# Source blocks of a graph kernel: packing ahead, four banks for the counts, aggregation in three parts

## What is computed

```python
# layer 0, three rounds: sum over neighbours, two linear maps
agg = segment_sum(x[src], dst); h = (1 + eps[i]) * x + agg
h = relu(bn(h @ W1[i] + b1[i])); h = relu(bn(h @ W2[i] + b2[i])); x = bn(h)
# layer 1: per edge, then mean over dst
h = relu(concat([x[row], edge_attr]) @ W1 + b1) @ W2 + b2
g = relu(concat([x, scatter_mean(h, col)]) @ W3 + b3) @ W4 + b4
# layer 2: attention over edges; layer 3: typed messages, normalised
```

## Time and profile before

| | us |
|---|---|
| median of 3 runs (lowest, highest) | 2091.39 (2090.84, 2094.32) |
| the profiled execution | 2095.73 |
| its span in the trace | 2094.4 |
| TensorE busy, share of the span | 1366.7, 65% |
| GpSimd busy | 790.0, 38% |
| VectorE busy | 1133.6, 54% |
| ScalarE busy | 601.6, 29% |
| mean granted TensorE clock (1.0 is 2.4 GHz) | 0.827 |

### The profile page before, as it was taken

One profiled execution on the slowest core, in us unless ns is written; L12 is line 12 of the kernel. 1 busy time (PEld: TensorE's weight loads), 2 busy tenths in 40 slices (PEclk: granted clock), 3 DMA queues, 4 the chain that ended last, 5 costly groups with the idle time before them and its releaser, 6 DMA issues.

```text
span 2094.4 us, 49695 instructions
## 1 busy us (share of the span) xinstructions
PE 1366.7 (65%) x20608; PEld 1258.3 (60%) x20609; DVE 1133.6 (54%) x3435; ACT 601.6 (29%) x1403; POOL 790.0 (38%) x881
## 2 busy tenths in 40 slices
PE   5103200011004777777899899999799999889997
PEld 5101200010003566666689799999789999789896
DVE  8104101110003666666544756655588888888987
ACT  0000000000003565555421344444356666500000
POOL 2771777777770000000000144444000011189886
PEclk9999555555555776677799899999899999899999
DMA  7301300001013766767475578888466664244443
GB/s 223 117 14 41 106 15 15 15 14 45 14 32 142 280 266 246 269 266 266 190 285 215 199 283 313 301 313 297 170 249 236 221 250 136 99 151 169 156 175 98
DMA packets 89288, 360.78 MB, mean 172 GB/s; under 512 B 24941, under 2 KB 38432, under 8 KB 82080
## 3 DMA queue, kind: packets, MB, share of 16 engines
q1 hardware_dynamic: 75744, 349.84, 45.1%
q0 software_dynamic: 13312, 7.69, 1.6%
HBM read 250.77 MB, written 106.68 MB: 171 GB/s over the span
## 4 chain that ended last, share of the span: by engine, by line
PE 47%; another core or an unknown queue 17%; issue 13%; DVE 12%; ACT 8%; POOL 2%; DMA 1%; SPq 0%; DVEq 0%; ACTq 0%; POOLq 0%
PE ps L2573 9%; PE ps L2921 7%; PE ps L2909 5%; PE ps L3540 5%; PE ps L3187 4%; PE ps L2463 3%; ACT arena L2530 2%; PE ps L3554 2%; PE ps L700 1%; PE ps L2389 1%; DVE arena L3605 1%; ACT arena L2475 1%; PE ps L2399 1%; DVE arena L3130 1%
## 5 line engine op out<-in xcount | busy, mean ns | idle before, releaser
L2194 POOL DMA_INDIRECT recs<-arena x416 | 415.1, 998 | 203.1 <-issue 126.6
L2979 POOL CAST arena<-arena 128x512 f32<-128x512 bf16 (+1 forms) x175 | 119.2, 683 | 733.2 <-DMA arena<-hot_out 563.7
L3540 PE MATMUL ps<-arena 125*128 125x64 bf16 x5850 | 192.5, 194 | 13.2 <-issue 13.1
L3540 PEld LDWEIGHTS ps<-arena 125*128 125x128 bf16 x5850 | 186.8, 99 | 14.4 <-issue 14.0
L2463 PE MATMUL ps<-wz,arena 32*128 32x128 f32 x1248 | 83.0, 381 | 164.6 <-ACT arena L2475 89.4
L2921 PE MATMUL ps<-arena 128*128 128x125 f32 x1300 | 182.2, 282 | 0.0
L3065 DVE TENSOR_TENSOR arena<-ps,arena 128x512 f32<-128x512 f32 (+1 forms) x175 | 114.3, 653 | 118.6 <-PE ps L2909 115.6
L2463 PEld LDWEIGHTS ps<-wz,arena 32*128 32x128 f32 x1248 | 68.9, 271 | 172.6 <-ACT arena L2475 90.9
L2921 PEld LDWEIGHTS ps<-arena 128*128 128x128 f32 x1300 | 158.8, 192 | 0.0
L2369 DVE TENSOR_SCALAR arena<-iota,arena 128x128 bf16<-128x128 bf16 x650 | 127.3, 253 | 50.7 <-issue 50.7
L3012 ACT ACTIVATE arena<-arena 128x512 f32<-128x512 f32 (+1 forms) x175 | 105.1, 601 | 171.7 <-DVE arena L3065 171.7
(11 more groups left out here) (381 smaller groups left out, 2692.3 us busy)
## 6 DMA issues: line engine op xcount, KB each, us to landing
arena<-ids_out SPq DMA_DIRECT2D x100, 832.0 KB, 6.4
arena<-hot_out SPq DMA_DIRECT2D x75, 832.0 KB, 6.3
arena<-e_out SPq DMA_DIRECT2D x25, 1664.0 KB, 7.0
arena<-adj_out SPq DMA_DIRECT2D x41, 800.0 KB, 6.2
e_out<-arena SPq DMA_DIRECT2D x25, 1024.0 KB
hot_out<-arena SPq DMA_DIRECT2D x25, 832.0 KB, 6.1
adj_out<-arena SPq DMA_DIRECT2D x25, 800.0 KB, 4.4
e_out<-arena SPq DMA_DIRECT2D x25, 640.0 KB, 3.2
```

The lines of the kernel that those rows point to most:

```text
L2194: nc.gpsimd.indirect_dma_start(out=recs, out_offset=bass.IndirectOffsetOnAxis(ap=slot_row[:, t:t + 1], axis=0), in_=rec_in[:, t, :], in_of ...
L2979: nc.gpsimd.tensor_copy(hot_e[s % NH][:, 0:len(js), :], hot_in[d % 2][:, js[0]:js[0] + len(js), :])\
L3540: ins = M(bank(step % 4, C, k * C), hot_r[d % 2][r][0:NP_, j * SLOTS:(j + 1) * SLOTS], px3[:, block_of(d, j), piece, r * C:(r + 1) * C], s ...
```

## The change

The order of work inside steps 0 to 24 is altered, and the PSUM banks of the counts. No computation is added or dropped.

- ACT packs block d+1 between the copies of e1's first and second half of block d (`act_pack`), and no longer at the head of step d+1. Only block 0 is packed at the head.
- The counts' seven groups lie in banks 4, 5, 2, 3, 4, 5, 2. Groups 0 and 1 wait only for the copies of the block before, 2 and 3 for the copies of the last e1, and 4 to 6 for groups 0 to 2.
- The transposes of block d wait for two of the four copies of the last half of e1 (banks 0 and 1), not for all four.
- `pe_z` of block d-1 is cut into 6, 12 and 7 matmuls: before e1's first half, between the halves, after the second. E1's first half now waits until all counts of block d are copied, since it writes banks 2 and 3.

```diff
@@ -2198,6 +2198,7 @@
 
         OPEN = 4
         READY = 5 * CH
+        Z_CUTS = (6, 18)
         LAST_E1 = 40
         DEGREES = 36
         STEPS = 26 * 2 + NT + 6
@@ -2380,7 +2381,7 @@
                     pe.wait_ge(sem("attr_packed"), d + 1)
                     if d >= 1:
                         pe.wait_ge(sem("attr_turned"), d)
-                        pe.wait_ge(sem("e1_made"), 8 * d)
+                        pe.wait_ge(sem("e1_made"), 8 * d - 2)
                     nc.tensor.transpose(bank(0, SLOTS)[0:3 * SB, :], idt[d % 2].rearrange("p k j -> p (k j)"),
                                         ident[:, :])
                     for g, js in enumerate(groups(d)):
@@ -2392,10 +2393,14 @@
                     for g in range(7):
                         n = 7 * d + g
                         pe.wait_ge(sem("hot"), n + 1)
-                        if n >= 2:
-                            pe.wait_ge(sem("adj_made"), n - 1)
+                        if g == 0 and d:
+                            pe.wait_ge(sem("adj_made"), 7 * d - 1)
+                        if g in (2, 3) and d:
+                            pe.wait_ge(sem("e1_made"), 8 * d)
+                        if g >= 4:
+                            pe.wait_ge(sem("adj_made"), 7 * d + g - 3)
                         for k, j in enumerate(sb_tiles(g)):
-                            to = bank(4 + n % 2, SLOTS, k * SLOTS)
+                            to = bank(ADJ_BANK[g], SLOTS, k * SLOTS)
                             ins = M(to, hot_s[d % 2][:, j, :], hot_d[d % 2][:, j, :], start=True, stop=j != d,
                                     skip_group_check=True)
                             if j == d:
@@ -2403,20 +2408,25 @@
                                         skip_group_check=True)
                         if g == 6:
                             for j in range(SB):
-                                ins = M(bank(4 + n % 2, 1, 256 + j), hot_d[d % 2][:, j, :], one16[:, 0:1], start=True,
+                                ins = M(bank(ADJ_BANK[g], 1, 256 + j), hot_d[d % 2][:, j, :], one16[:, 0:1], start=True,
                                         stop=True, skip_group_check=True)
                         ins.then_inc(sem("adj_mm"), 1)
-                if step < NT - 1:
-                    pe.wait_ge(sem("attr_turned"), step + 1)
-                    pe_e1_half(pe, step, 0)
                 if 1 <= step <= NT:
                     d = step - 1
                     pe.wait_ge(sem("adj_made"), 7 * d + 7)
                     pe.wait_ge(sem("z_read"), d)
-                    pe_z(pe, 0, d, range(NT))
+                    pe_z(pe, 0, d, range(Z_CUTS[0]))
+                if step < NT - 1:
+                    pe.wait_ge(sem("attr_turned"), step + 1)
+                    pe.wait_ge(sem("adj_made"), 7 * step + 7)
+                    pe_e1_half(pe, step, 0)
+                if 1 <= step <= NT:
+                    pe_z(pe, 0, step - 1, range(Z_CUTS[0], Z_CUTS[1]))
                 if step < NT - 1:
                     pe.wait_ge(sem("e1_made"), 8 * step + 4)
                     pe_e1_half(pe, step, 1)
+                if 1 <= step <= NT:
+                    pe_z(pe, 0, step - 1, range(Z_CUTS[1], NT))
                 for l in range(3):
                     pe_tail(pe, l, step)
                 for l in (1, 2):
@@ -2451,6 +2461,8 @@
                     pe.wait_ge(sem("deg_rows"), 1)
                     pe_e1_last(pe)
 
+        ADJ_BANK = (4, 5, 2, 3, 4, 5, 2)
+
         def e1_slots(half, r):
 
             return [j for j in range(16 * half, min(16 * half + 16, SB)) if j % 4 == r]
@@ -2463,6 +2475,14 @@
                     ins = M(bank(r, HID, (g - 4 * half) * HID), attT[rows, g * 128:(g + 1) * 128],
                             wz[rows, r * HID:(r + 1) * HID], start=True, stop=True, skip_group_check=True)
             ins.then_inc(sem("e1_mm"), 1)
+
+        def act_pack(act, d):
+
+            act.wait_ge(sem(f"block_in{d % 2}"), 16 * (d // 2 + 1))
+            act.wait_ge(sem("turned"), d)
+            A(attc.rearrange("p (j f) -> p j f", f=FE),
+              recd[d % 2].rearrange("p (j f) -> p j f", f=REC)[:, :, 4:REC], ACT.Copy)\
+                .then_inc(sem("attr_packed"), 1)
 
         def act_e1_half(act, d, half):
 
@@ -2502,11 +2522,8 @@
             for step in range(STEPS):
                 if step < NT:
                     d = step
-                    act.wait_ge(sem(f"block_in{d % 2}"), 16 * (d // 2 + 1))
-                    act.wait_ge(sem("turned"), d)
-                    A(attc.rearrange("p (j f) -> p j f", f=FE),
-                      recd[d % 2].rearrange("p (j f) -> p j f", f=REC)[:, :, 4:REC], ACT.Copy)\
-                        .then_inc(sem("attr_packed"), 1)
+                    if d == 0:
+                        act_pack(act, 0)
                     act.wait_ge(sem("turned"), d + 1)
                     if d >= 2:
                         act.wait_ge(sem(f"ids_stored{d % 2}"), 16 * (d // 2))
@@ -2526,11 +2543,12 @@
                         m = len(sb_tiles(g))
                         act.wait_ge(sem("adj_mm"), n + 1)
                         if g == 6:
-                            A(present[:, d, :], bank(4 + n % 2, SB, 256), ACT.Copy)
-                        A(adj[d % 2][:, 4 * g:4 * g + m, :].rearrange("p s n -> p (s n)"), bank(4 + n % 2, m * SLOTS),
+                            A(present[:, d, :], bank(ADJ_BANK[g], SB, 256), ACT.Copy)
+                        A(adj[d % 2][:, 4 * g:4 * g + m, :].rearrange("p s n -> p (s n)"), bank(ADJ_BANK[g], m * SLOTS),
                           ACT.Copy).then_inc(sem("adj_made"), 1)
                     if d < NT - 1:
                         act_e1_half(act, d, 0)
+                        act_pack(act, d + 1)
                         act_e1_half(act, d, 1)
                 for l in range(3):
                     act_tail(act, l, step)
```

## The result

| | changed | before |
|---|---|---|
| median, same chip (lowest, highest) | 2010.35 us (2007.65, 2013.39) | 2091.11 (2090.78, 2094.32) |
| ratio, 95% interval | 0.9611 (0.9594, 0.9628) | |
| profiled execution; its span | 2007.65; 2006.3 | 2095.73; 2094.4 |
| start of block 1's transposes | 644.29 | 652.28 |
| a step, mean of 23 | 12.76 | 16.08 |

The change takes 3.9%, some 81 us, where 72 were forecast. The two profiled spans differ by 88.1 us: 8.0 before block 1, 76.3 in the 23 steps, 3.8 behind them. (In one of the five sets of runs the chip was of another kind: the kernel before takes 1655 us on it, and the change, seen there together with an earlier load alone, brings nothing. The experiments come to it.)

What follows compares the result with a forecast made beforehand. A chain across engines, PE and ScalarE taking turns, was taken to set the 16.08 us step. Summed terms gave 13.0: 23 steps save 70.8 us, the start 1.5, so 2091.39 - 72.3 = 2019.1 us; range 1996 to 2050.

Steps and rivals of the forecast that it cites:

- a step of 13.0: Steps between block 1's and block 24's transposes: 16.08 us falls to 13.0, with ends of 11.5 and 14.2.
- a sign of being wrong: In the steps: the forecast is wrong if PE's first part of the aggregation waits for VectorE's reading.
- the six aggregation matmuls: Ahead of e1's first half: six matmuls of the aggregation fill PE's wait, with no term in the step's sum.
- The packing: ScalarE's instruction between e1's copies and the transposes: 0.80 us leaves the chain, covered by 0.89 idle.
- The four banks: Copies of counts: six already run without a gap, 3.46 us; 0.58 gained at the end is given back; net nothing.
- E1's first half: PE's e1 matmuls in each step: 1.8 us, from 2.02 at the low clock to 1.42 at the high one.
- Rival A: In the steps, the block's load or VectorE becomes late: 13.9 us a step, 2039 us; chance 0.22.
- B: First block beside the scatter: e1's first matmul waits for ScalarE's copies, overlap lost, +85 us, 2104; chance 0.03.
- C: In the steps, the clock stays high: step 11.5 to 12.0, DMA and VectorE begin to bind, 1991 us; chance 0.10.
- D: In the steps, nothing happens, since another wait of the same length stands right behind; chance 0.02.
- The start: Block 1's transposes, at 652.28, could begin after two copies, at 649.98 + 0.8: 1.5 us more gained.
- 14.2: Low-clock end of the step in us, with mean tail; by the rule on cycling PSUM banks the step would go there.

## Why the prediction was right, by its own steps

**The number, and the luck in it.** The forecast had 72 us and 2019; the ratio gives 81 and 2010. The turns of PE and ScalarE that the change takes apart were the right mechanism, which undoing each part shows. But a step of 13.0 was summed over these turns alone, with VectorE 2.2 us early, and in the changed kernel VectorE's reading holds PE up in 14 of 22 steps, which the forecast itself had named as a sign of being wrong. Where that wait is gone, with the load early, the same turns give 11.76, at a clock of 0.93. So the sum was some 1.2 us too long, the wait that it left out was worth 1.0 with the clock that goes with it, and the two nearly cancel: that the step came out at 12.76 is in part luck.

**The sum of the step.** 13.0 forecast (its terms give 13.07), 12.76 measured. Its terms in the step from 784.40 to 796.95: transposes 1.1 (forecast 1.5; 1.05 was the low end); copies of them 1.1 (1.07); six copies of counts 3.0 (3.46); group 6's copies 0.4 (0.4), in part beside the six aggregation matmuls; e1's first half 2.07 (1.8); four copies 2.1 (2.06); e1's second half 0.95 (0.95); the rest until the next transposes 1.1 (1.45). One term stands there that the sum had at nothing: the six aggregation matmuls, 0.9. The transposes with the ids came out at 0.28 to 0.31 in every step but the first, so the clock was up there each time.

**Three terms mis-sized.** *The packing*: I priced it at its own 0.80 a step, 18 us, in the expectation of its run; alone it brings 53, 2.3 to 2.4 us a step. 1.1 of them are PE's shorter wait before the transposes, for part of the tail of ScalarE that stood between copies and packing (0.64) leaves the chain too. The clock rises from 0.73 to 0.86, which I take for the rest: after shorter pauses PE has its high clock more often. No run held the clock fixed, so that share is argued, not shown. The prediction's step total had both in, as a range. *The four banks*: "ScalarE gains nothing within them" was wrong. A merged row of the timeline hid the gaps: six copies take 3.01 instead of 3.46, 0.45 a step, 10 us. The chain of waits of the kernel before had shown 0.14 and a piece of PE's work after every second copy, and I should have gone by it. *E1's first half* at the high clock takes 1.17 (676.58 in the changed kernel), below my low end of 1.42, which I had scaled from the second half.

**The parts don't add.** The packing alone brings 53; the other parts without it 58; together 81. Undoing any one costs 17 to 24. With any one part missing the step is 13.6 to 13.7, at clocks from 0.76 to 0.85; with all it is 12.8, and there the late load and VectorE behind it stop it.

**Rival A** (0.22) is what happened as a mechanism, though not at its price: PE's first part waits for VectorE's reading in 14 of 22 steps. I had VectorE's reading 2.2 us early at a step of 13.0 and late only if the load grew. The load did not grow in the median (3.5 us in both kernels); what went is my slack, since the chain without VectorE is shorter than 13.0. A's price was a mean step of 13.9; nine steps are of 13.5 to 16.7 and the others 11.0 to 12.7, so that the mean stayed near the forecast. The early load took 25 us, more than the 20 between A's price and the forecast. **B** fell: ScalarE's copies come at 500.48 and 589.38 in the changed kernel, 88.9 apart (before 89.0), so PE's new wait cost nothing. **C** was not reached by the change, but the early load reached its step (11.8) and its time (1989 against 1991). The prediction's **D**, no gain, fell with the ratio.

**The start.** 1.5 us were forecast and 8.0 measured. Of these 1.3 are the change's: the transposes of block 1 start 1.0 us after e1's copies begin (643.28), before 2.3 (649.98). The other 6.7 stand in ScalarE's copies already, and 14.3 in its small copy of group 6 (500.48, before 514.77), ahead of which nothing of the change but the banks comes. Over the ten profiles of crawling chips that small copy starts anywhere from 499 to 515, whatever the kernel, and block 1 from 643.8 to 652.3. I take the 6.7 as spread.

**The clock and the banks.** The rule of the Trainium skill that I weighed (TensorE: Matmul & The Clock Gate, "A second HAM failure mode: psum-queue depth-cycling") speaks of cycling through banks. Here four banks gave the higher clock (0.88) and two the lower (0.80), with e1's added wait the only other difference, and the step did not go to 14.2. Nor does the number of banks order the clock over all runs: four banks with the aggregation in one piece have 0.76, two banks with the packing moved 0.86. So the rule is not borne out in this kernel. What makes the clock fall is not settled. From 670 to 900 us of the changed kernel it falls eleven times in some 18 steps, ten times before e1's first half begins and once 0.1 us after. In the step shown it falls in the midst of the six aggregation matmuls, at 790.0, after pauses of PE of 0.90, 0.32 and 0.50 us, and e1 begins at 790.55; PE alone, clock in the third column from the end:

```profile
789.90:790.00 0.10, 0.10 (x4) 0.94 0.55 225
790.00:790.10 0.10, 0.10 (x4) 0.50 2.19 646
```

E1's first half took 2.09 us in all 23 steps before; in the changed kernel it takes 1.17 where the clock stays up.

**What was missed altogether** is that the crawl of the first block is no property of the kernel. I took it as given, and the whole worth of the change hangs on it: where PE does not crawl, the steps hide beside the scatter. On that chip the changed kernel ran only with the load early or with the wait for the scatter, and two of its parts alone.

**The version that beats both** is the changed kernel with the load early, 0.9490 of the kernel before and, on the other kind of chip, 1.0007, no loss.

**Open.** What makes PE crawl in four of the five sets of runs, and what ends it, at 643 to 650, when the copies of e1's second half begin. It begins beside the scatter and outlives it, and the program is the same on all. How much of the gain is the clock's. The aggregation in parts alone was not run on a crawling chip, the four banks alone on none, and the transposes' wait for two copies was never undone by itself.

## What to carry to other kernels

When two engines take turns, price a moved instruction by everything that stands between the two hand-overs, and reckon with PE's clock: here 0.8 us of instruction was worth 2.4, 1.1 of it in the shorter wait. A forecast for one loop is also a claim on every other loop: sum those too, here from the copies of e1 over the stores, the load and VectorE back to PE, and at the shortest step that the first loop could reach. Look at what the faster step fills: here the DMA engines at 0.70 had room for a store, and at 0.89 they hadn't. The load that everyone waits for should stand ahead of the stores that nobody waits for. And look which stretch of the kernel the profile's own chip makes long: a change in it can be worth 4% on one chip and nothing on the next.

## What the runs showed of the hardware

The same program takes 1655 us on one chip and 2090 to 2097 in four other sets of runs. In these four the first block's matmuls take 1.2 to 2.8 us each, where the other chip does twenty in 1.7 us, so its blocks can't run beside the scatter. PE's records can stand long before their work reaches the next engine: 20 matmuls recorded within 1.65 us set ScalarE going 24 us after the first. I read that as a queue ahead of PE, but the rows don't tell it from a late signal. In such a stretch go by ScalarE's rows, not PE's.

A load's time from issue to first use stayed at 3.5 us in the median when the DMA engines went from 0.70 to 0.89 busy, and rose to 4.4, at most 8.1, at 0.96 with one more store of 832 KB a block. TensorE's granted clock fell before small row-tiled matmuls began, not in them, in ten of eleven falls (changed kernel, 670 to 900 us).
